# Experts of a two-layer kernel: low parts and weight splits on POOL, V later in the first stage, five waits and constants placed elsewhere

## The reference

```python
# layer 0, cross attention: 16 heads of 64, keys that are all zero are masked
scores = einsum('bhsd,bhdn->bhsn', q, k) * scale
x = x + (softmax(where(mask, -inf, scores)) @ v) @ Wo        # input: layernorm(x)
# layer 0, experts: 8 experts of width 512, and a shared one
scores = softmax(xf @ gate_weight.T).T                       # (8, 2048)
vals, idx = top_k(scores.reshape(-1), 2 * 2048)              # the 4096 largest of all
y = einsum('esf,efd->esd', gelu(xf @ W1 + b1), W2) + b2
x = x + sum over e of gate[e] * y[e] + shared(xf)            # input: layernorm(x)
# layer 1, cross attention, one head, keys cos(K Wr + br)
x = x + softmax(Q @ K_hat) @ V
# layer 1, feed-forward: base product, shared low rank, 6 routed low ranks with the top 2 weights
x = x + base_out + shared_out + routed_out
```

## Time and profile before

| | us |
|---|---|
| median of 3 runs | 1993.79 (1993.67 to 1994.15) |
| the profiled execution | 1994.03 |
| its span, first to last instruction | 1992.3 |
| TensorE busy | 1869.9 |
| VectorE busy | 1309.1 |
| POOL busy | 1200.3 |
| ScalarE busy | 1122.4 |

### The profile page before, as it was taken

The page is one execution under the profiler, slowest core; times in us unless marked ns, Lnnn a source line. Parts: engine busy times, 40 slices in busy tenths (PEclk is TensorE's granted clock), DMA queues, the critical chain, the costliest instruction groups (busy, mean ns, idle before and its releaser), DMA issues. The chain is left out here.

```text
span 1992.3 us, 42221 instructions
## 1 busy us (share of the span) xinstructions
PE 1869.9 (94%) x16013; PEld 1454.6 (73%) x16013; DVE 1309.1 (66%) x3449; ACT 1122.4 (56%) x1616; POOL 1200.3 (60%) x680
## 2 busy tenths in 40 slices
PE   6999999999999999999999999999988899869996
PEld 4777777777777777777777777777766588657775
DVE  6566667666656766676666657666635677867765
ACT  4555555555555555555555555555557699644443
POOL 4666666666666666666666666667766355424441
PEclk9999999999999999999999999999998899979998
DMA  3000000000000000000000000000000222022210
GB/s 102 2 1 18 1 4 18 1 2 4 18 1 4 2 18 2 4 18 1 2 4 18 2 5 2 7 6 2 1 1 22 86 86 81 9 62 67 69 50 22
DMA packets 56414, 41.21 MB, mean 21 GB/s; under 512 B 2516, under 2 KB 53660, under 8 KB 55196
## 3 DMA queue, kind: packets, MB, share of 16 engines
q1 hardware_dynamic: 56220, 38.57, 6.7%
HBM read 37.45 MB, written 1.11 MB: 19 GB/s over the span
## 5 line engine op out<-in xcount | busy, mean ns | idle before, releaser
L597 POOL TENSOR_TENSOR a_den<-a_den,a_probs 128x1024 f32<-128x1024 f32 x352 | 838.5, 2382 | 385.4 <-ACT a_probs L847 384.4
L847 ACT ACTIVATE a_probs<-a_scores,a_mask_col 128x1024 f32<-128x1024 f32 x416 | 463.6, 1114 | 557.0 <-PE a_scores L727 515.9
L963 DVE CUSTOM_DVE_ANT_0 a_work<-a_work,a_mask_row 128x400 f32<-128x400 f32 (+1 forms) x1024 | 567.7, 599 | 213.9 <-PE a_work L637 210.6
L743 PE MATMUL a_pv<-a_probs,a_V 128*64 128x256 f32 x3328 | 406.0, 386 | 0.0
L743 PEld LDWEIGHTS a_pv<-a_probs,a_V 128*64 128x64 f32 x3328 | 220.8, 137 | 126.4 <-issue 25.3
L727 PE MATMUL a_scores<-a_shiftT,a_pick 64*128 64x256 f32 x1664 | 236.5, 277 | 0.0
L727 PEld LDWEIGHTS a_scores<-a_shiftT,a_pick 64*128 64x128 f32 x1664 | 161.1, 186 | 0.0
L963 DVE DVE_READ_ACCUMULATOR2_ANT a_maxes<- 128x1 f32 x1024 | 144.2, 141 | 0.0
L723 PE MATMUL a_scores<-a_Q_hi,a_K_hi 64*128 64x256 f32 x832 | 127.1, 300 | 9.7 <-ACT a_probs L847 9.5
L1164 DVE TENSOR_TENSOR m_h_lo<-m_h,m_h_hi 128x512 fp32r<-128x512 f32 x120 | 104.6, 884 | 44.8 <-ACT m_h_hi L1423 44.3
L826 ACT ACTIVATE a_V<-a_work 128x512 f32<-128x512 f32 (+1 forms) x224 | 124.7, 568 | 14.2 <-PE a_work L617 6.6
(11 more groups left out here) (386 smaller groups left out, 4106.2 us busy)
## 6 DMA issues: line engine op xcount, KB each, us to landing
m_gate_rows<-gate_scratch SPq DMA_DIRECT2D x8, 1024.0 KB, 4.9
a_c_nat<-in_ctx_dram SPq DMA_DIRECT2D x8, 768.0 KB
b_c_in<-in_ctx_dram SPq DMA_DIRECT2D x8, 768.0 KB
b_c_nat<-in_ctx_dram SPq DMA_DIRECT2D x8, 768.0 KB
m_w_raw<-in_L_ffn_W_dram SPq DMA_DIRECT2D x16, 256.0 KB, 5.0
a_acc<-in_x_dram SPq DMA_DIRECT2D x8, 128.0 KB, 2.1
out_dram<-tokens SPq DMA_DIRECT2D x4, 256.0 KB, 2.5
tokens<-in_x_dram SPq DMA_DIRECT2D x1, 896.0 KB, 9.4
```

Source lines behind the costliest of these rows:

```text
L597: nc.gpsimd.tensor_tensor(total, so_far, probs[:, buffer(c, j), :], ALU.add).then_inc(den_added, 1)
L743: last = nc.tensor.matmul(PV[HD * odd:HD * odd + HD, c % 2, queries], V[:, c % 2, j, h * HD:(h + 1) * HD], probs[:, buffer(c, j), first:fi ...
L847: nc.scalar.activation(probs[:, buffer(c, j), :].rearrange("p (o n) -> p o n", o=2), Sc[:, :, :], ACT.Exp, bias=mask_col[:, c // GROUPS % ...
L963: nc.vector.tensor_tensor_reduce(out=X[:, bank, :w], in0=X[:, bank, :w], in1=mask_row[:, off:off + w], scale=1.0, scalar=-3e38, op0=ALU.ad ...
```

## The change

In attention_0, the V products of stage 0 go to later slots (V_FIRST), and in stages that load and scan a context, the spread transposition goes behind one of two K products rather than ahead of both. In moe_0, POOL makes the low parts of 30 steps and not of 24; the four splits of the weights of experts 1 and 2 stand behind low parts 5 and 9 of stages 0 and 1; and in stage 8 the additions stand ahead of what finish_turns(2) does. In attention_1 the bias products of a projection stand ahead of the wait and of the weights' products, and the statistics of two more tiles are taken in the last stage. In ffn_1 TensorE's wait for POOL's constants stands later, and those two tiles' statistics are gone.

```diff
@@ attention_0
+    V_FIRST = (0, 0, 1, 2, 2, 1, 1)
...
-        for w, n in enumerate(V_AT[c % GROUPS]):
+        for w, n in enumerate(V_AT[c % GROUPS] if c > 0 else V_FIRST):
...
-            middle[wides[5]].insert(0 if c % 2 else len(middle[wides[5]]), (s, "spread", 0))
+            middle[wides[5]].insert(len(middle[wides[5]]) if c % 2 == 0 else 1 if has_context(c + 1) else 0, (s, "spread", 0))
@@ moe_0
-    POOL_CUTS = STEPS + 8
+    POOL_CUTS = STEPS + 14
+    SPLITS_AT = {(0, 5): (1, 0), (0, 9): (1, 1), (1, 5): (2, 0), (1, 9): (2, 1)}
...
                     for k in range(max(0, min(STEPS, POOL_CUTS - c * STEPS))):
                         cut(nc.gpsimd, pool, it, c, k)
-                if 0 < c < E:
+                        if (c, k) in SPLITS_AT:
+                            split(None, *SPLITS_AT[c, k])
+                if 1 < c < E:
                     for n in range(2):
                         split(it, c + 1, n)
...
                     for tg in range(TG):
-                        if c == E and tg > 0:
-                            finish_turns(tg - 1)
                         cols = acc[:, tg * 512:(tg + 1) * 512]
                         pool.wait_ge(y_taken, at(it, 2 * TG, c * TG + tg + 1))
                         pool.wait_ge(added, at(it, 2 * TG, (c - 2) * TG + tg + 1))
                         nc.gpsimd.tensor_tensor(cols, cols, gated[:, tg % 2, :], ALU.add).then_inc(added, 1)
+                        if c == E and tg < 2:
+                            finish_turns(tg)
                 if c == E and it is None:
+                    finish_turns(2)
                     finish_turns(3)
...
-            for n in range(2):
-                split(None, 1, n)
             experts(pool, body)
@@ attention_1
         if c == STAGES - 1:
+            slots[11].append(("fstat", EARLY // 2))
...
                 elif kind == "proj":
+                    for j in range(2):
+                        nc.tensor.matmul(out[:, j * D:(j + 1) * D], ones[0:1, :], bv_row[:, :], start=(j == 0), stop=False,
+                                         skip_group_check=True)
                     pe.wait_ge(norm_done, at(it, 2, c))
                     for j in range(2):
-                        half = out[:, j * D:(j + 1) * D]
-                        nc.tensor.matmul(half, outT[:, j * P:(j + 1) * P], w_raw[:, 3, :], start=True, stop=False)
-                        last = nc.tensor.matmul(half, ones[0:1, :], bv_row[:, :], start=False, stop=True)
+                        last = nc.tensor.matmul(out[:, j * D:(j + 1) * D], outT[:, j * P:(j + 1) * P], w_raw[:, 3, :],
+                                                start=False, stop=(j == 1), skip_group_check=True)
@@ ffn_1
             pe.wait_ge(FT.loaded, 128)
-            pe.wait_ge(consts, 1)
             nc.tensor.transpose(A[:, 0, 0:ROWS], small[:, :], ident[0:ROWS, 0:ROWS])
...
+            pe.wait_ge(consts, 1)
             for g in range(2):
                 routed_products(g, A[:, g, :])
...
-            for t in LAST_TILES:
+            for t in LAST_TILES[2:]:
                 link(nc.vector.bn_stats(parts[:, t, :], XS[:, t, :]))
```

## The result

The changed kernel takes 1983.65 us (median of 5 runs, 1982.45 to 1985.45) against 1993.79 us (median of 5, 1992.73 to 1994.15): a ratio of 0.995, 95% interval 0.9937 to 0.9963, 10.1 us faster. The profiled execution took 1983.65 us, its span is 1981.9 us, 10.4 us under the one of before. In the lines shown, those of kernel.py have moved by 1 to 6.

The account below looks back on a forecast made before the run. TensorE, busy 94% of the span, was taken as the bound, held up by a loop of waits in the search. Terms -10.6+1.6-0.4+3.2+1.8-1.6-1.4-1.05-0.5 = -8.95 us from 1994.03 gave 1985.1, adjusted to 1984.8 (1983.3 to 1986.5, chance 0.50).

Parts of the forecast that it names:

- The search: Experts' first stages: low parts 24 to 29 on POOL end a loop of waits; gates' transpose 10.6 us earlier.
- The turns: Token selection before the gates' transpose: three two-input VectorE instructions each wait for a POOL low part, 3.2 us lost.
- The clock behind the transpose: Experts, behind the gates' transpose: TensorE's clock drops after a 4.3 us wait, costing 1.8 us (bounds 0 and 4).
- The end of the experts: Last addition to acc moved ahead of finish_turns(2): it and TensorE's transposes come 1.6 us sooner.
- The transposition: First attention: a K product ahead of the wait for the spread transposes gains 0.5 us once, 0 in six other stages.
- V: First attention, stage 0: later V products can only fill waits; taken as 0, bounds 1.5 us either way.
- The other projections: Second attention, projections before the last: bias products moved ahead gain 0, as TensorE is full either way.
- The last projection and the last part: End of second attention: bias products ahead of the wait gain 1.4 us; last part's first copy comes 1.05 us sooner.
- Rival (a): Token selection: no turns between VectorE and POOL, or too few to drop the clock; 1979.8 us, chance 0.30.
- Rival (b): Experts: the clock stays low longer, costing 4 us, and V costs 1.5 us; 1988.5 us, chance 0.12.
- rival (c): Experts: POOL becomes the bound and is slower than before; 1998.3 us at 1.90 us a low part, chance 0.02.
- rival (d): Experts' search: the loop of waits stays because low parts behind splits come a step late; 1990.4 us, chance 0.04.

Follow-up runs that it names:

- cuts_alone: The kernel before with only POOL_CUTS changed, so POOL also makes low parts 24 to 29: 1985.78 us, ratio 0.996.
- spread_back: The changed kernel with the spread transposition placed as in the kernel before: 1983.61 us, ratio 0.9946 to before.
- last_part_back: splits_28 with the last part as before (constants awaited ahead of the first transposes, all four statistics there): 1979.09 us, ratio 0.9927 to before.
- splits_28: spread_back with the two splits of expert 2 behind low parts 20 and 28 rather than 21 and 25: 1978.67 us, ratio 0.9922 to before.
- late_splits: The changed kernel with both splits of expert 2 behind low part 29: 1985.07 us, ratio 0.9955 to before.
- v_alone: The kernel before with only the later V products of stage 0 of the first attention: 1995.14 us, ratio 1.0009.

## Why the prediction held, and where it did not

Its total was 1984.8 us against 1983.65 measured, but four of its terms are off by more than 1 us, in both directions.

**The search.** Right. Without the turns the changed kernel's stretch to the transpose is 10.64 us shorter (8.25 and 2.39), for 10.6 forecast, and 11.05 in cuts_alone, which has no split ahead of low part 22. Up to the 25th gelu 1.35 us were lost for 1.6. Of these, 1.0 us is low part 10 (1.01 to 1.05 us between the 11th and the 15th gelu in all eight traces with both splits there, 0.5 in the two with one, none in the others); the 0.3 us ahead of it is not there in spread_back and last_part_back. Of the signs, no low part of VectorE ahead of step 30 and the clock came; the wait in front of product 10 is 0.75 us and not 1.6, and the transpose came 7.0 us earlier for "about 6". The splits of expert 2 ended 10 us ahead of step 32 (1552.2 and 1562.3), not twenty as I wrote; splits_28 takes part of that room.

**The turns.** The mechanism was right, its size 2.39 us for 3.2: I added the length of a low part to each instruction, but the 1.25 us that a waiting instruction takes hold its own 0.29 us, so a whole turn costs 0.96, 0.94 and the half one 0.48. I had named L1502 to L1504 of before as the ones to wait; it was L1500, L1502 and L1503 (now L1503, L1505, L1506), for POOL's queue ran dry before the last. The instruction that I had passed over has one input tensor in SBUF and waited too, 0.77 for 0.29 us. The Trainium skill (SBUF — State Buffer, Who interferes with whom) says that tensor_scalar can take the shared ports as well, if its operands allow the mode for it; I had used only its rule on two inputs. The trace agrees with the rule (1.25 and 1.23 us) and doesn't contradict the other (0.77 us); no row shows in which mode the instruction ran.

**The clock behind the transpose.** 1.8 us forecast, 1.4 us found (the distance of the two traces shrinks from 7.04 to 5.63 us by the 32nd gelu). That it comes from the wait, cuts_alone, late_splits and splits_28 show: at 1.20 us of waiting there is none right behind it.

**The end of the experts.** 1.6 us forecast, 1.67 us found from the last gelu to the transposes of acc. Another 0.48 us was gained between the 32nd and the last gelu (0.60 lost by the 41st, 1.15 gained by the 51st), which I can't attribute to an edit.

**The transposition.** The step that failed most clearly, in its sign. I priced the wait in front of it, 0.83 us in one stage, and wrote that in the six other stages "there is no wait, so 0". The wait was behind it: the next stage's first scores need ScalarE's copy of the transposed shift. Ahead of both K products that copy was done at 136.86 us, 0.15 us before the scores; between them it stands behind a K copy and ends at 137.79, and the scores go at 137.89 (the program lets the first scores of a stage wait for this copy; the view gives no releaser). So +1.56 us rather than -0.5. The trace of before had it: that copy ended 0.15 us ahead of the scores.

**V.** 0 forecast, 0.2 us lost in every trace that has it.

**The other projections.** "TensorE is full either way; I take 0" missed that the edit also regroups the products: 1.55 us gained.

**The last projection and the last part.** 3.00 us were gained up to its first product, for 2.45 forecast, and 2.16 us lost behind it, 1.82 of them up to the last addition. I counted no clock there, though the page of before has it low in this stretch, and 2.5 us more of the low stretch lie behind that product now (5.9 for 3.4).

**The first attention's end.** 1.58 us of the gain in this pair of traces is a low stretch that one has and the other has not. I had not counted it; whether the change's delay of the last stage has a part in it stays open.

Without that last item the pair of traces would differ by 8.8 us. That the sum stood so near is in part that a miss of 2.1 us (transposition) and one of 2.2 us (last part) met one of 1.55 us (projections), one of 1.58 us (the low stretch), 0.85 us in the turns and 0.94 us up to acc: luck, as far as the terms go. Rival (a), no turns, is refuted by the trace of the changed kernel, and shown as a kernel of its own by splits_28. Rival (b) falls, since the low stretch behind the transpose lasted 3.4 us; rival (c), since the 30 low parts took 1.29 us on average and none over 1.31; rival (d), since the loop is gone.

## What to carry to other kernels

When a step is moved, look for who waits behind it as well as for what it waits for: the price was on the reader's side, once in ScalarE's queue and once in a wait for both splits. Work that an engine must do sometime goes where that engine stands idle for another reason, here between two low parts while TensorE waits for the gates, and not merely early or late. And idle time taken out of a stretch at half clock can be worth only part of its length, if the low stretch then reaches further into the work.

## What the runs showed of the hardware

A TENSOR_SCALAR of VectorE with one input tensor took 0.77 us beside a POOL subtraction and 0.29 alone; a TENSOR_TENSOR with one of two inputs in PSUM took 0.29 us beside one too. In the other direction POOL's cast of a weight took 1.07 us beside VectorE's low parts and 0.61 alone. Alternating products over 128 rows and over one row cost 0.2 us for each change (an estimate from two orders). TensorE's clock fell or not near the same place of nearly the same code, for 1.6 us. Behind the first product of the last part each microsecond of low clock cost 0.7 us, in 14 traces. From the transposes of acc to the 13th exponential v_alone took 1.6 us less than before with the same code there. And the launch itself moves everything by up to 2.3 us (first exponential at 46.07 to 48.36 us).
